# A fused attention and mixture-of-experts block: weights split in the projections, and four token groups of the shared expert at the end

## The reference

```
x = x + LN( attention( LN(x) ) )
    attention: h = LN(X)*w + b;  Q, K, V = h @ W_in + b_in;  Q, K rotated (RoPE, first half)
               A = sum over tokens of (K / |K|) * V        (one row per sequence)
               (A * Q) @ W_out + b_out + X
x = x + LN( ffn( LN(x) ) )
    ffn: logits = n @ gate_w;  the two best of 8 experts, softmax over their logits
         routed = sum gate_e * ( gelu(n @ w1[e] + b1[e]) @ w2[e] + b2[e] )     (512 -> 256 -> 512)
         shared = gelu(n @ shared_w1 + shared_b1) @ shared_w2 + shared_b2      (512 -> 512 -> 512)
         routed + shared
```

## Time and profile before

| what | value |
|---|---|
| median of three runs | 1028.24 us (1027.85 to 1035.12) |
| the profiled execution, its time | 1027.98 us |
| its span in the trace | 1025.8 us |
| TensorE busy | 896.8 us, 87% |
| VectorE, ScalarE, POOL busy | 628.3, 442.0, 404.4 us |
| mean granted TensorE clock | 0.95 |
| DMA | 174.68 MB, 170 GB/s |

### The profile page before, as it was taken

How to read it: one execution, slowest core, us unless ns; L and a number is a source line. 1 busy time by engine, 2 the same in 40 slices (tenths; PEclk the granted TensorE clock), 3 DMA queues, 4 the chain that set the end, 5 groups by cost and what they waited for, 6 DMA issues and landing times.

```text
span 1025.8 us, 14729 instructions
## 1 busy us (share of the span) xinstructions
PE 896.8 (87%) x4562; PEld 739.3 (72%) x4562; DVE 628.3 (61%) x1356; ACT 442.0 (43%) x830; POOL 404.4 (39%) x337
## 2 busy tenths in 40 slices
PE   1999999999997699999999748499999999969883
PEld 1877787787785467777778537488988988857662
DVE  5656766676664775656665587366665666655653
ACT  4134233433423124122242645366666666653462
POOL 3356446545631400000000000277677777730464
PEclk9999999999998889999999878799999999989886
DMA  9122644545337568645424650678778878789496
GB/s 314 45 81 105 244 143 161 188 158 200 135 144 306 190 239 312 227 165 215 154 83 169 215 151 32 238 144 149 140 147 163 154 146 149 147 176 350 62 160 107
DMA packets 78074, 174.68 MB, mean 170 GB/s; under 512 B 10841, under 2 KB 19289, under 8 KB 73137
## 3 DMA queue, kind: packets, MB, share of 16 engines
q1 hardware_dynamic: 52096, 124.60, 33.6%
q0 software_dynamic: 20592, 45.96, 25.1%
q10 hardware_dynamic: 5312, 3.18, 1.3%
HBM read 103.68 MB, written 80.53 MB: 180 GB/s over the span
## 4 chain that ended last, share of the span: by engine, by line
PE 70%; DVE 11%; issue 7%; ACT 4%; POOL 3%; DMA 2%; SPq 1%; POOLq 0%; ACTq 0%; DVEq 0%
PE bank L1434 12%; PE bank L1435 12%; PE bank L1436 12%; PE bank L1626 3%; PE bank L1628 3%; PE bank L1627 3%; PE bank L1643 3%; PE bank L1645 3%; PE bank L1644 3%; PE bank L1613 3%; PE bank L1429 3%; POOL out L1413 2%; DVE we L1061 2%; PE bank L1635 2%; ACT hb L535 1%
## 5 line engine op out<-in xcount | busy, mean ns | idle before, releaser
L1385 POOL DMA_INDIRECT f_scratch<-ro,dst x71 | 113.2, 1595 | 48.7 <-SPq L513 23.2
L1377 POOL DMA_INDIRECT xr<-n_scratch,ids x72 | 71.1, 987 | 90.9 <-issue 65.6
L1434 PE MATMUL bank<-wkv_hi,h_hi 128*128 128x512 f32 x256 | 101.1, 395 | 3.8 <-issue 3.8
L1436 PE MATMUL bank<-wkv_hi,h_lo 128*128 128x512 f32 x256 | 100.7, 393 | 0.0
L1435 PE MATMUL bank<-wkv_lo,h_hi 128*128 128x512 f32 x256 | 100.6, 393 | 0.0
L1188 DVE TENSOR_TENSOR ro<-bank,b2b 128x512 f32<-128x512 f32 x71 | 49.1, 692 | 70.3 <-PE bank L1645 70.3
L1626 PE MATMUL bank<-we,x_hi 128*128 x284 | 86.4, 304 | 0.0
L1628 PE MATMUL bank<-we,x_lo 128*128 x284 | 80.7, 284 | 0.0
L1627 PE MATMUL bank<-we,x_hi 128*128 x284 | 80.6, 284 | 0.0
L544 ACT ACTIVATE sq<-kb 128x512 f32<-128x512 f32 x32 | 20.3, 633 | 134.2 <-DVE kb L845 134.2
L1344 POOL TENSOR_TENSOR zr<-zv,half 128x4 f32<-128x4 f32 x8 | 8.1, 1009 | 137.7 <-DVE zv L961 137.7
(11 more groups left out here) (232 smaller groups left out, 2514.2 us busy)
## 6 DMA issues: line engine op xcount, KB each, us to landing
xg<-in_X SPq DMA_DIRECT2D x16, 1024.0 KB, 9.1
q_scratch<-qh SPq DMA_DIRECT2D x8, 1024.0 KB, 3.9
q_scratch<-qb SPq DMA_DIRECT2D x8, 1024.0 KB, 7.1
expert_scratch<-in_w SPq DMA_DIRECT2D x16, 512.0 KB, 7.1
q_hi<-q_scratch SPq DMA_DIRECT2D x8, 1024.0 KB, 4.7
q_lo<-q_scratch SPq DMA_DIRECT2D x8, 1024.0 KB, 6.9
out<-z SPq DMA_DIRECT2D x8, 1024.0 KB, 5.1
n_scratch<-n SPq DMA_DIRECT2D x8, 1024.0 KB, 6.4
```

What stands on the lines that cost most here:

```text
L1377: pool.indirect_dma_start(xr[u][:, :], None, n3_dram, bass.IndirectOffsetOnAxis(ids[:, i:i + 1], 0)).then_inc(row_in[u], 16)
L1385: pool.indirect_dma_start(f_dram, bass.IndirectOffsetOnAxis(dst[:, i:i + 1], 0), ro[i % NRO][:, :], None, compute_op=ALU.add).then_inc(r_s ...
L1434: pe.matmul(dst, hi(k), w_hi(k), start=(k == 0), stop=False)
L1436: last = pe.matmul(dst, lo(k), w_hi(k), start=False, stop=(k == KD - 1 and not more))
```

## The change

Four things are changed together.

1. The experts' and the shared expert's weights are split while the projections run. They are 20 units of 128 x 1024 elements, each loaded into one of two buffers `w_lo`, copied to `w_hi` by ScalarE (`unit_hi`), subtracted by VectorE (`unit_lo`), and stored as a high and a low part in DRAM. Groups 1 to 5 take four units each, one after each K tile. Later stages load both parts and split nothing.
2. The bias of the output product (`bo`) is made ready in group 0 and not where attention begins.
3. EARLY is (0, 3, 6, 7), so four groups are late. The fillers are h0, o0, h3, o3, h6 in steps 1, 2, 4, 5 and 7. f is zeroed in step 0 instead of step 2.
4. The end's first loads wait until the first gathers are through, its transposes use four banks in place of two, and loads and normalisations stand in another order.

The tables of numbers:

```
-EARLY = (1, 3, 5, 6, 7)
+EARLY = (0, 3, 6, 7)
...
-        fill = {2 + i: (("h", "o")[i % 2], EARLY[i // 2]) for i in range(6)}
+        fill = {1: ("h", 0), 2: ("o", 0), 4: ("h", 3), 5: ("o", 3), 7: ("h", 6)}
...
-        normed_in = beside((0, 0, 0, 0, 0, 0, 0, 0, 0, 1, 1, 1, 2, 2, 2, 2, 1, 1, 1, 1, 2, 1, 1, 1))
+        normed_in = beside((0,) * 6 + (1,) * 16 + (0,) * 10)
```

SyncE in the projections:

```
-            def copy_expert(e):
+            def load_unit(u):
+                if u >= len(units):
+                    return
+                if u >= 2:
+                    sp.wait_ge(w_stored[u % 2], 32 * (u // 2))
+                w, k = unit_in(u)
+                sp.dma_start(w_lo[u % 2][:, :].bitcast(F32).rearrange("p (k h) -> p k h", k=k), w).then_inc(raw_w_in[u % 2], 16)
+
+            def store_unit(u):
+                sp.wait_ge(unit_split, u + 1)
+                for c, w in ((0, w_hi), (1, w_lo)):
+                    sp.dma_start(unit_out(u, c), w[u % 2][:, :].bitcast(F32)).then_inc(w_stored[u % 2], 16)
...
             for g in range(NG):
+                u = UG * (g - 1)
+                with_units = 0 <= u < len(units)
                 sp.wait_ge(h_normed, g + 1)
                 load_x(g + 2)
+                if with_units:
+                    store_unit(u)
+                    load_unit(u + 2)
                 if g >= 1:
                     store_q(g - 1)
+                if with_units:
+                    store_unit(u + 1)
+                    load_unit(u + 3)
+                    store_unit(u + 2)
+                    load_unit(u + 4)
                 if g + 1 < NG:
                     sp.wait_ge(k_rotated, GT * (g + 1))
                     load_rt(g + 1)
                     sp.wait_ge(q_rotated, g + 1)
                     load_rf(g + 1)
-                if 1 <= g <= 4:
-                    copy_expert(2 * g - 2)
-                    copy_expert(2 * g - 1)
...
+                if with_units:
+                    store_unit(u + 3)
+                    load_unit(u + 5)
```

ScalarE in the projections:

```
+            def unit_hi(u):
+                act.wait_ge(raw_w_in[u % 2], 16 * (u // 2 + 1))
+                if u >= 2:
+                    act.wait_ge(w_stored[u % 2], 32 * (u // 2))
+                act.activation(w_hi[u % 2][:, :], w_lo[u % 2][:, :].bitcast(F32), ACT.Copy).then_inc(unit_hi_done, 1)
...
                     norm_k(g, j)
                     if j == 1 and g >= 1:
                         q_hi_parts(g - 1)
+                    if 0 <= UG * (g - 1) < len(units):
+                        unit_hi(UG * (g - 1) + j)
                 if g + 1 < NG:
                     front_split(g + 1, (g + 1) % 2)
```

VectorE in the projections:

```
+            def unit_lo(g, j):
+                u = UG * (g - 1) + j
+                if 0 <= u < len(units):
+                    dve.wait_ge(unit_hi_done, u + 1)
+                    dve.tensor_tensor(w_lo[u % 2][:, :], w_lo[u % 2][:, :].bitcast(F32), w_hi[u % 2][:, :].bitcast(F32), ALU.subtract)\
+                       .then_inc(unit_split, 1)
```

In attention and routing:

```
-                if s == 2:
+                if s == 0:
                     sp.wait_ge(consts_set, F_ZERO)
...
-            def load_expert(e):
-                for i in range(2):
-                    sp.dma_start(we[:, e, 2 * i + 1, :].bitcast(F32), we_dram[e, i]).then_inc(we_in[e], 16)
+            def load_expert(e, parts=range(4)):
+                c = slice(parts[0], parts[-1] + 1)
+                sp.dma_start(we[:, e, c, :].bitcast(F32), we_dram[e, c].rearrange("c p h -> p c h")).then_inc(we_in, 16)
...
-            expert_lo((5, 1, 2, 6))
...
-                if b in (4, 7, 10, 13):
-                    f_out(7, (b - 4) // 3)
-                if b == 9:
-                    expert_lo((7,))
+                for j in {2: (0, 1), 5: (2,), 8: (3,)}.get(b, ()):
+                    f_out(7, j)
```

At the beginning of the end stage:

```
             sp.wait_ge(dst_ready, 1)
-            sp.dma_start(n3c[0][:, :, :], n3_groups[LATE[0]]).then_inc(n3c_in[0], 16)
-            sp.dma_start(c_raw[0][:, :, :].rearrange("p k h -> p (k h)"), ws_dram[0]).then_inc(s_in[0], 16)
+            sp.wait_ge(xt_full, 2 * NX)
+            load_n3(0)
+            sp.dma_start(c1_hi[:, :, :].rearrange("p k h -> p (k h)").bitcast(F32), ws_dram[0, 0]).then_inc(c_in[0], 16)
```

More of the change, by code:

```diff
@@ L97, in sandwich_kernel @@
         upper_at = kept[0]
-        upper, ones_f = keep("upper", [P, P]), keep("ones_f", [P, P])
+        upper, ones_f = keep("upper", [P, P]), keep("ones_f", [P, P], F32R)
         pick = keep("pick", [P, E])
@@ L142, in sandwich_kernel @@
         wo_lo = [at("wo_lo0", 136, [P, KD, D], F32R), at("wo_lo1", 8, [P, KD, D], F32R)]
+        UW = KD * H
+        UG = 4
+        units = [(e, i, 0) for e in range(E) for i in range(2)] + [(E + i, 0, h) for i in range(2) for h in range(2)]
+        w_lo = [at(f"w_lo{i}", 128 + 4 * i, [P, UW], F32R) for i in range(2)]
+        w_hi = [at(f"w_hi{i}", 136 + 4 * i, [P, UW], F32R) for i in range(2)]
         rc, rsn = at("rc", 144, [P, 2, G]), at("rsn", 148, [P, 2, G])
@@ L228, in t2_use @@
             return (KD + 1) * g + k
-        fill = {2 + i: (("h", "o")[i % 2], EARLY[i // 2]) for i in range(6)}
-        assert all(fill[s][1] == s - 1 for s in (2, 4, 6))
+        fill = {1: ("h", 0), 2: ("o", 0), 4: ("h", 3), 5: ("o", 3), 7: ("h", 6)}
+        assert all(fill[s][1] == s - 1 for s in fill if fill[s][0] == "h")
         o_order = []
@@ L431, in _ @@
             sp.wait_ge(q_rotated, NG)
-            sp.wait_ge(ws_copied, 32)
-            load_s(1, s2_lo)
             store_q(NG - 1)
+            for u in range(2):
+                sp.wait_ge(w_stored[u], 32 * len(units) // 2)
             sp.wait_ge(q_stored[1], 32 * NG // 2)
             load_q(1)
-            load_s(0, s1_lo)
+            load_s(0, (s1_hi, s1_lo))
+            load_s(1, (s2_hi, s2_lo))
             def store_f(g, j):
@@ L498, in _ @@
               .then_inc(bias_in[0], 16)
-            for j in range(GT):
+            for j in range(GT - 1):
                 store_f(7, j)
@@ L513, in _ @@
                 sp.sem_inc(r_landed, 1)
-            for n, g in enumerate(f_loads):
-                sp.dma_start(f[g][:, :, :], f_groups[g]).then_inc(f_in[n // 2], 16)
+            load_f(EARLY[0])
+            load_n3(1)
+            load_f(EARLY[1])
+            load_f(LATE[0])
+            load_f(EARLY[2])
+            load_n3(2)
+            load_f(EARLY[3])
+            load_f(LATE[1])
+            load_n3(3)
+            load_f(LATE[2])
+            load_f(LATE[3])
             sp.wait_ge(stored, 16 * NT)
@@ L599, in _ @@
                     keep_acol(0)
+                if g == GB + 2:
+                    for u in range(2):
+                        act.wait_ge(w_stored[u], 32 * len(units) // 2)
                     scale_wo(0)
@@ L782, in _ @@
                     gelu_c(i, m)
-                for g, j in y_of[what, i, m]:
-                    normed(g, j)
                 if what == "h" and m == KS - 1 and i + 1 < len(LATE):
@@ L787, in _ @@
                         nc_hi_part(i + 1, k)
+                for g, j in y_of[what, i, m]:
+                    normed(g, j)
             normed(*y_order[-1])
@@ L1554, in shared_o @@
                 n = o_use["o", g, j]
+                if g == h_order[0] and j == 0:
+                    pe.wait_ge(s_in[1], 32)
                 pe.wait_ge(hs_split, h_use(g, KS - 1) + 1)
```

243 lines of the change are left out of this document (107 added, 136 removed).

## The result

The changed kernel takes 1072.36 us in the median of four runs (1072.02 to 1073.79), the kernel before beside it 1029.28. The ratio is 1.041, with a 95% interval of 1.038 to 1.045. The profiled execution took 1072.24 us, its span is 1070.4. The forecast was 1067 us and a span of 1064.8.

The account below looks back on a forecast made before the run. TensorE was taken to bound the projections and the chain through VectorE the routing. Span 1025.8 + 80 (front) - 18 (attention) - 23 (routing) + 0 (end) = 1064.8, with 2.2 added 1067 us; range 1015 to 1088.

Parts of the forecast that it names:

- The sign and the mechanism: Whole kernel slower, 3.8%; in the projections five hb waits of some 14 us behind a unit copy's load, then half clock.
- front: Projections, groups 1 to 5: 14 us of stall and 2 of slow clock each, +80 us, between 40 and 102.
- the end: From the first product to the last instruction: unchanged, 0 us, between -3 and +12, keeping 6.6 of some 20 us of waits.
- the round trip of unit 2: Projections, group 2: store landed by 132.1, unit 4's load by 136.3, so hb starts at 137.4 and not 123.26.
- The slower clock: Projections, behind each of five stalls: TensorE at half clock, 2 us a group, between 1 and 3.5, 10 us together.
- the four subtractions: Projections, each group with units: 4 x 1.22 us on VectorE hidden in the stall or beside matmuls; otherwise hb some 3 later.
- Attention: Attention stage: -18 us, between -30 and -10; net -5 from start-up gains less transfer delays, -13.5 from fillers.
- the backlog: Attention, step 0: 16 MB of transfers delay ScalarE's n of step 1, costing 6 us and 2 for the clock.
- Routing: Routing stage: -23 us, from -38 to -15; no gain before f tile (6,2), then splitting, marker stretch and a wait shrink.
- The third part: Routing, second gathered tile: TensorE's 4.50 us wait goes, as the end's first loads no longer stand beside the gathers.
- my own signs of being wrong: hb within 8 us of the last k tile, routing under 85 us, or the end growing by 10.
- The tail: End, after the last f: 10 us in place of 17, as early tiles' writes no longer queue.

Follow-up runs that it names:

- Experiment 1: Changed kernel with ScalarE's fourth unit copy behind the bias of q and VectorE's fourth subtraction behind the moments: 1024.81 us, ratio 0.995.
- experiment 2: Changed kernel with SyncE's unit 2 store and unit 4 load ahead of the two q stores: 1055.60 us, ratio 1.025.
- kernel 12: Changed kernel with reordered unit slots, q's low part ahead of the fourth K tile, f stores first, zeros in group 6, end loads reordered: 997.05 us, ratio 0.968.
- 8: Changed kernel with kernel 12's front order, but the units' 20 subtractions left out and raw weights stored as low parts: 1006.52 us, ratio 0.978.
- Experiment 5: Changed kernel with the 5 MB of zeros for f stored in group 6 of the projections, not in attention: 1061.97 us, ratio 1.035.
- experiment 6: Changed kernel with two units split earlier, q's low part behind the fourth K tile, fourth copy between q biases, units stored ahead of q: 1023.61 us, ratio 0.998.

## Why the prediction was right, point by point

**The sign and the mechanism** held. hb waits five times, ScalarE idles until a load lands, and the clock is at half behind it. Experiment 1 moved only that copy and its subtraction and took back 49 of the front's 70 us, experiment 2 only the queue's order and took back 18.

**The total is nearer than its parts.** 1067 against 1072 is partly luck: the front came out 10 us lower than forecast, the end 11 higher, and the expert loop, which had no term, 4 higher.

**Front, +80 against +70.** One size was off, the round trip of unit 2. The three MB from the first q store to unit 2 were there in 144.56 - 134.72 = 9.84 us; I had 11.1 from the two landing times of q and 3.6 for a further MB. Up to the end of the projections TensorE's waits for hb grew by (67.9 - 8.1) / 5 = 12.0 us a group, not 14; some 0.7 us of that difference is not traced. The slower clock cost 291.2 - 281.3 = 9.9 us by TensorE's busy time, where I had 10. One thing the forecast did not have: it wrote that the four subtractions lie within the stall. In the changed kernel they do. Without it they cost 6.6 us (kernel 12 against 8), where the forecast had some 3 us a group, 15, on hb. The Trainium skill, TensorE: Matmul & The Clock Gate, Part 1, would have taken the clock's 10 us off. The 9.9 us measured are under 1% of the span, as it says; but each gap has its slow stretch, and in a sum that has to tell 1% they belong in it. The Trainium skill, DMA: Bandwidth & Descriptors, Specifications, would, by the prediction's estimate, have put the front at 61 and not 80; the measured 70 lies halfway.

**Attention, -18 against -19.2**, and both parts are in place: the first turn 14.1 earlier, the steps 5.1 shorter with ScalarE's 8.66 us for n's store. Experiment 5 prices the backlog at 5.8 us.

**Routing, -23 against -21.5, with two errors that cancel.** f tile (6,2) comes 45.98 us after the z tile and not at 50.85: from the store of x2 at 599.14 the 13 MB took 38.7 us, 3.0 us a MB and not 3.3. The first marker is then 15.7 us earlier, where I had 9.9. But from the markers to the ids the time fell from 29.04 to 26.9, by 2.1, and I had 8.6. I had counted VectorE's instructions there; it also waits for TensorE's o tiles (5.1 us in four waits) and marker products, 2.57 us at the last, with TensorE's clock at half (0.51) from 669 to 690. The third part, the wait of 4.50 us at the second gathered tile, went as forecast.

**The step that failed is the end: 0 was forecast, +10.9 measured**, just inside the bound of 12, and past one of my own signs of being wrong ("if the end grows by 10"). Its first product comes 4.0 us sooner after the turn (forecast 3.2). From there to the last f are 108.3 us and not 99.8: of the 20 us of waits and slow clock I kept a third, and 15 remained. The windows between these marks and TensorE's waits in them say which, first the kernel before:

```profile
920.00:1009.00 89.00, 78.16 (x320) 62.94 (x319) 52.82 (x142) 41.19 (x62) 34.37 (x42) 0.89 0.79 184
PE bank L1429 <- DVE nc_lo L1211: 6.3, 2, 4.4
PE bank L1434 <- DVE hc_lo L1216: 3.5, 1, 3.5
```

```profile
949.00:1058.00 109.00, 97.94 (x432) 79.41 (x432) 60.47 (x162) 48.98 (x74) 38.30 (x48) 0.97 0.81 200
PE bank L1450 <- DMA n3c<-n_scratch: 4.5, 1, 4.5
PE bank L1455 <- DVE hc_lo L1258: 3.8, 3, 2.2
PE bank L1704 <- ACT hsc L783: 1.9, 3, 0.8
```

The slow clock went (0.89, now 0.97), and so did the waits for nc_lo, 6.3 us, that the four banks and the split were about. But others came in their place: waits were 10.5 us in all, with 0.7 for hsc, and are 10.2. The largest is the load of the second n: TensorE waits 4.50 us, and the turn takes 3.56 at half clock and not 1.94. The tail is 12.9 us and not 10. Loading that n earlier cost elsewhere; in the best order the end was still 123.5 us. So a fourth late group still costs some 9 us there.

**The expert loop, +4.3, had no term.** Twelve of its tiles take 3.8 to 4.5 us and not 3.5, with ScalarE's hg late; in the kernel before seven took 3.6 to 3.8. From the first gathered tile to the end's first turn the kernels of the experiments took 256.5 to 263.6 us, around the 260.3 of the kernel before. Why is open.

## What to carry to other kernels

When work is fitted beside a busy engine, find the engine whose result that one waits for, and keep every wait for a transfer off its list ahead of that result: the position of one copy and its subtraction was worth 47 us, and all the bytes and copies together 2 in the projections. When one wait is gone, look for the next: in experiment 6 the wait for hb was back at its old size and the loss stood at the bias of q. A round trip (store, then reload into the same buffer) has the price of everything that its queue has ahead of it, so store first what a reload waits for. And an idle stretch of VectorE is a place for work on SBUF only if POOL's work in it can wait.

## What the hardware showed that I had not expected

Two elementwise operations on SBUF, one on VectorE and one on POOL, did not slow each other by a share here; one waited until the other was over: 3.27 us and not 1.22, ended 1.1 us after POOL's operation. The changed kernel shows it too: unit 2's subtraction in group 2, beside an accumulation of POOL that ended at 135.84, took 2.30 us and ended 1.1 us after it. And the same 5 MB of zeros cost 5.8 us, 7.8 or nothing, by which store stands behind them.
